# Moving one output-projection tile, the token statistics and the last rope copies to other places in a fused attention and FFN kernel

## What is computed

```python
xn = layernorm(x)
s = attention(xn)        # 16 heads of 32, rope on q and k, causal softmax, output projection Wo
g = silu(ffn(xn))        # bitlinear(w_fc) -> gelu -> bitlinear(w_proj), ternary weights
out = x + s * g
```

## Time and profile before

| what | value |
|---|---|
| median of 3 executions | 1184.5 us (1182.86 to 1184.88) |
| the profiled execution, its own time | 1183.88 us |
| its span, first to last instruction | 1182.2 us |
| PE busy | 1140.4 us, 96% |
| DVE busy | 846.1 us, 72% |
| ACT busy | 792.0 us, 67% |
| POOL busy | 520.4 us, 44% |
| mean granted TensorE clock | 0.999 of full speed |

### The profile page before, as it was taken

How to read it: one execution, slowest core, us unless ns; L and a number is a source line. 1 busy time by engine, 2 the same in 40 slices (tenths; PEclk the granted TensorE clock), 3 DMA queues, 4 the chain that set the end, 5 groups by cost and what they waited for, 6 DMA issues and landing times.

```text
span 1182.2 us, 20037 instructions
## 1 busy us (share of the span) xinstructions
PE 1140.4 (96%) x7580; PEld 559.3 (47%) x7580; DVE 846.1 (72%) x1442; ACT 792.0 (67%) x1492; POOL 520.4 (44%) x894
## 2 busy tenths in 40 slices
PE   4989999999999999999999999999999999999997
PEld 3555545446444454445544454444544445444553
DVE  6988848797558875588547984479745887558854
ACT  4787974578826868269663797447873587826964
POOL 2135442572526625275243744257252562526434
PEclk9999999999999999999999999999999999999999
DMA  8490001910128000450007401092001900045011
GB/s 302 152 125 21 2 29 38 141 55 1 30 30 149 19 3 28 56 123 19 30 1 85 94 19 30 1 122 75 2 30 24 155 19 4 27 53 91 19 39 37
DMA packets 52587, 67.31 MB, mean 57 GB/s; under 512 B 9353, under 2 KB 34313, under 8 KB 51977
## 3 DMA queue, kind: packets, MB, share of 16 engines
q1 hardware_dynamic: 52488, 66.02, 28.3%
HBM read 31.98 MB, written 8.40 MB: 34 GB/s over the span
## 4 chain that ended last, share of the span: by engine, by line
PE 71%; DVE 15%; ACT 6%; POOL 3%; issue 2%; DMA 1%; SPq 1%; POOLq 0%; DVEq 0%; ACTq 0%
PE banks L404 22%; PE banks L561 17%; PE banks L530 12%; PE banks L648 5%; PE banks L617 5%; ACT arena L847 4%; PE banks L509 4%; DVE arena L1104 3%; DVE mix L1080 3%; DVE arena L1102 3%; PE banks L516 2%; DVE mix L983 1%; PE banks L434 1%; ACT banks L825 1%; POOL mix L1290 1%
## 5 line engine op out<-in xcount | busy, mean ns | idle before, releaser
L561 PE MATMUL banks<-projT,arena 128*128 128x512 f16 x1024 | 285.3, 377 | 0.0
L825 ACT ACTIVATE banks<-banks,mix,scl 128x512 f32<-128x512 f32 (+2 forms) x384 | 249.4, 668 | 15.5 <-POOL mix L1290 14.1
L1080 DVE TENSOR_REDUCE mix<-banks 128x1 f32<-128x384 f32 (+3 forms) x352 | 218.9, 637 | 35.9 <-PE banks L516 20.0
L530 PE MATMUL banks<-xT,fcT 128*128 128x512 f16 x1024 | 228.4, 379 | 0.9
L847 ACT ACTIVATE arena<-banks,scl 128x1280 f32<-128x1280 f32 x128 | 164.7, 1328 | 68.9 <-PE banks L617 65.5
L1273 POOL TENSOR_TENSOR split_buf<-xr_buf,split_buf 128x512 f16<-128x512 f32 x64 | 74.0, 1177 | 247.2 <-ACT split_buf L771 247.2
L1282 POOL TENSOR_TENSOR xh_buf<-xh_buf 128x512 f32<-128x512 f32 x120 | 152.3, 1269 | 65.6 <-ACT xh_buf L794 61.9
L404 PE MATMUL banks<-xT,qkT 128*128 128x512 f16 x768 | 168.7, 379 | 0.0
L530 PEld LDWEIGHTS banks<-xT,fcT 128*128 128x128 f16 x1024 | 97.7, 98 | 121.9 <-ACT xh_buf L794 9.8
L1290 POOL TENSOR_SCALAR mix<-mix,scl 128x1 f32<-128x1 f32 (+1 forms) x288 | 76.2, 265 | 153.9 <-DVE mix L1080 144.4
L1053 DVE TENSOR_TENSOR arena<-banks,mix 128x512 f32<-128x512 f32 x128 | 79.4, 682 | 85.1 <-PE banks L404 85.1
(11 more groups left out here) (152 smaller groups left out, 1570.4 us busy)
## 6 DMA issues: line engine op xcount, KB each, us to landing
stacks<-split_buf SPq DMA_DIRECT2D x192, 128.0 KB, 5.1
out_dram<-arena SPq DMA_DIRECT2D x32, 256.0 KB, 3.0
xr_buf<-in_L_attn_x_dram SPq DMA_DIRECT2D x7, 1024.0 KB, 7.2
resid<-in_L_attn_x_dram SPq DMA_DIRECT2D x28, 256.0 KB, 5.0
stacks<-in_L_ffn_w_fc_dram SPq DMA_DIRECT2D x1, 4096.0 KB, 25.2
arena<-in_L_ffn_w_proj_dram SPq DMA_DIRECT2D x1, 4096.0 KB, 14.5
mix<-norm_row SPq DMA_DIRECT2D x8, 256.0 KB, 3.9
xr_buf<-in_L_attn_x_dram SPq DMA_DIRECT2D x4, 256.0 KB, 4.1
```

The costliest lines, as they stand in the source:

```text
L530: mm = pe.matmul(banks[:, UP_BANKS[f % NUB], :], fcT[:, c, f * P:(f + 1) * P], xT[:, part, c, :], start=(c == 0 and part == 0), stop=(c == ...
L561: mm = pe.matmul(banks[:, 6 + t % 2, :], lhs, projT[:, f, :], **ends)
L825: mm = nc.scalar.activation(block, block, ACT.Exp, scale=col(EXP_SCALE), bias=exp_bias[:, i, h0 + k:h0 + k + 1], accum_out=row_sum[:, i, h ...
L1080: nc.vector.tensor_reduce(row_max[:, i, h0:h0 + n], scores_of(r), AX_X, ALU.max).then_inc(max_ready, 1)
```

## The change

It alters when things are issued. No matmul is added or left out. One output tile more (tile 1) goes from `out_projection` to `late_out_projection`, so the queue beside the rounds holds 36 output matmuls in place of 24, and `GIVEN` is worked out anew with a lead of 17 and 20 behind rounds 3 and 4 (batch 0 keeps the old lead). Tiles 1, 2, 3 are scaled behind rounds 4, 7 and 12. POOL adds x to each in two halves, behind rounds 6 and 7, 9 and 10, 14 and 15. The statistics of the next batch stand behind the maxima of rounds 5, 7, 9 and 11, and are joined behind round 12, in batch 0 too. POOL's ten steps start at round 16. In all batches but the first, the last rope pair's copies stand behind GELU 2.

```diff
-OUT_EARLY = 2
+OUT_EARLY = 1
 OUT_BESIDE_SCORES = (NT - OUT_EARLY) * OUT_MATMULS
-STATS_AFTER = (8, 9, 10, 11)
-FIRST_STATS_AFTER = (9, 10, 11, 12)
+LATE_STATS_AFTER = {5: 0, 7: 1, 9: 2, 11: 3}
-NORM_FROM = 8
+NORM_FROM = 16
...
-DOWN_LEAD = (0, 0, 11, 13, 16)
+FIRST_LEAD = (0, 0, 11, 13, 16)
+LEAD = (0, 0, 11, 17, 20)
...
-RESIDUAL_AFTER = {r + 2: t for r, t in SCALED_AFTER.items()}
+RESIDUAL_AFTER = {r + 2 + half: (t, half) for r, t in SCALED_AFTER.items() for half in range(2)}
...
-                    pe.wait_ge(scaled_ready, b * NT + t - 1)
+                    if t >= 2:
+                        pe.wait_ge(scaled_ready, b * NT + t - 1)
...
-                    if f == 0:
+                    if f == (0 if first else 2):
                         split_rotated(3)
...
-                    stats_after = FIRST_STATS_AFTER if first else STATS_AFTER
-                    if f in stats_after and not last:
-                        token_statistics(b + 1, stats_after.index(f))
-                    if f == FC - EARLY - 1 and not last:
-                        join_statistics(b + 1)
...
                 for r in range(EARLY, NR):
                     maxima(r)
+                    if r in LATE_STATS_AFTER and not last:
+                        token_statistics(b + 1, LATE_STATS_AFTER[r])
+                    if r == NORM_FROM - 4 and not last:
+                        join_statistics(b + 1)
...
+            def add_half_of_x(b, t, half):
+
+                cols = slice(half * D // 2, (half + 1) * D // 2)
+                pool.wait_ge(resid_dma[t % 2], b * 32 + 16 * (t // 2) + 16)
+                pool.wait_ge(scaled_ready, b * NT + t + 1)
+                added = nc.gpsimd.tensor_tensor(result[:, t, cols], result[:, t, cols], resid[:, t % 2, cols], ALU.add)
+                if half:
+                    added.then_inc(result_ready, 1)
...
-                    for t in range(2):
+                    for t in range(OUT_EARLY):
                         add_x(b - 1, t)
...
-                        add_x(b - 1, RESIDUAL_AFTER[r])
+                        add_half_of_x(b - 1, *RESIDUAL_AFTER[r])
```

More of the change, by code:

```diff
@@ L64, with given_after_rounds @@
 EXP_COLS = [sum(n * ((i + 1) * P + 412) if i else 940 for i, _, n in ROUNDS[:r + 1]) for r in range(NR)]
-DOWN_LEAD = (0, 0, 11, 13, 16)
-def given_after_rounds(total):
-    return [DOWN_LEAD[r] if r < NSB else DOWN_LEAD[-1] + (total - DOWN_LEAD[-1]) * EXP_COLS[r - NSB] // EXP_COLS[-1] for r in range(NR)]
+FIRST_LEAD = (0, 0, 11, 13, 16)
+LEAD = (0, 0, 11, 17, 20)
+def given_after_rounds(lead, total):
+    return [lead[r] if r < NSB else lead[-1] + (total - lead[-1]) * EXP_COLS[r - NSB] // EXP_COLS[-1] for r in range(NR)]
 def round_behind(given, matmuls):
     return 1 + min(r for r in range(NR) if given[r] >= matmuls)
-FIRST_GIVEN = given_after_rounds(DOWN_BESIDE_SCORES)
-GIVEN = given_after_rounds(OUT_BESIDE_SCORES + DOWN_BESIDE_SCORES)
+FIRST_GIVEN = given_after_rounds(FIRST_LEAD, DOWN_BESIDE_SCORES)
+GIVEN = given_after_rounds(LEAD, OUT_BESIDE_SCORES + DOWN_BESIDE_SCORES)
 FIRST_KEEP_DOWN = tuple(round_behind(FIRST_GIVEN, (t + 1) * DOWN_MATMULS) for t in range(2))
```

## The result

The changed kernel takes 1188.54 us (median of 7, 1187.27 to 1189.17) against 1183.78 us of the kernel before, run beside it. The ratio is 1.0037, with a 95% interval of 1.0025 to 1.0049: slower. The prediction said 1189.3 us against 1184.5, a ratio of 1.0041.

What follows compares the result with a forecast made beforehand. PE, busy 1140.4 of 1182.2 us, was taken as the bound, so only its stalls count. Batches 1 to 6 +3.2, batch 7 +0.7, batch 0 +0.9: +4.8 us, 1189.3 against 1184.5; range 1182.5 to 1193.5, the forecast's own 1186.5 to 1192.

Steps and rivals of the forecast that it cites:

- The forecast case: Whole kernel: 1189.3 us against 1184.5, 0.4% slower, by the sum of PE's stalls; chance 0.60.
- (a): Up projection to round 0, before the change: PE loses 0.38 us per batch, put down to statistics on DVE.
- (b): Round 4, before the change: 0.82 us late per batch, released by a square, put down to statistics on DVE.
- The moved tile at zero: Batches 1 to 7: 12 matmuls (2.59 us) move from ahead of the up projection to beside the rounds; zero by itself.
- Copies behind GELU 2: Up tile 4, batches 1 to 7: the copies make tile 1's square late on ACT, +0.83 us each.
- Stalls (a) and (b) gone: Batches 1 to 6: with the statistics out of the up projection both stalls vanish, together -1.20 us per batch.
- DVE in the pass: Score pass, rounds 4 to 13: 10.2 us of DVE work makes round 18 late, 0.9 us lost per full batch.
- POOL: Score pass: half additions, steps and powers delay biases; 0.9 us lost at round 22, 0.2 from the power at round 21.
- rival 1: Score pass: DVE's backlog is absorbed and the pass's old 1.11 us stall falls to zero; 1176 us, chance 0.10.
- Batch 0: First batch: +0.9 us at round 18, +0.2 by later powers, -0.2 in the up projection; +0.9 in all.
- The transfer of x's tile 3: Load issued about 539.2, landing 4.1 us later, before POOL wants it at 545.1; covered by 1 to 2 us.
- The port rule: Statistics beside POOL's halves might block on a shared port; charged nothing. With a late transfer as rival: +4, 1193, chance 0.13.

Runs made afterwards that it cites:

- run 7: The change with rope copies apart behind two squares, statistics behind rounds 17 to 23, POOL's steps from 28, but output tile 1 and lead put back: 1176.0 us.
- run 8: The kernel before with only the last rope pair's copies moved behind GELU 2: 1200.0 us, ratio 1.0136.
- run 1: The change with the last rope pair's two copies apart, behind the squares of tiles 0 and 1, in all batches but the first: 1183.14 us.
- run 2: The change with only POOL's ten layer-norm steps moved, from round 16 to round 28: 1181.46 us, ratio 0.9977.
- run 3: The change with only the statistics and their join put back in the up projection, behind tiles 8 to 12 (batch 0: 9 to 12): 1186.24 us.
- run 9: The change with both rope copies behind GELU 0 again in every batch: 1189.04 us, ratio 1.0041.

## Why the prediction was right

The forecast case came true, with its mechanism. The range, 1182.5 to 1193.5, held the time, and so did the forecast's own, 1186.5 to 1192. The medians differ by 4.8 us, as forecast. That this agrees to a tenth is partly luck, since single terms are off by about 0.1 us per batch in both directions. Taken from the two traces, the six full batches lose 3.4 us (forecast 3.2), batch 0 1.05 (0.9) and batch 7 0.65 (0.7), 5.1 us of span.

- *Bound.* PE has the same matmuls, so the time moved by PE's stalls. The period came to 141.30 us where 141.2 was said. A full batch is longer by 0.57 us on average, and the stalls of PE down to 0.04 us account for 0.54 of it: +0.83 at tile 4, -1.20 for (a) and (b), and +0.91 in the pass (2.03 for 1.12).
- *The moved tile at zero.* Nearly right for its matmuls (0.16 us in run 7). What I had not priced is that POOL's addition of x moves with it. The kernel before has no stall at tile 7, so there was nothing to win against it. But with the copies behind GELU 2 the moved addition is what keeps tile 7 on time: without it 0.50 us more would be lost in each of seven batches (run 8). The sum had no such term, and that this was right is luck, since the prediction never worked out tile 7.
- *Copies behind GELU 2,* +0.83 us. Measured 0.83 in six of the seven batches (0.28 and 0.55 at tiles 3 and 4 in batch 3, where a rope transfer was late), and by taking it away, 5.4 of 5.8 us (run 1, where 0.26 us at tile 3 of batch 3 remain).
- *Stalls (a) and (b) gone,* -1.20 us. Both are gone. The earlier trace rows shows rounds 3 and 4 of batch 7, and not 4 and 5 as its title and the prediction say: two output matmuls stand between them, and three behind round 4. So the 0.16 us of batch 7 are round 4's own stall without statistics, and of (b)'s 0.82 only 0.66 belong to the statistics; run 7, with the old lead and no statistics there, loses the same 0.16. The sum doesn't change.
- *DVE in the pass,* +0.9. Measured 0.19 + 0.07 + 0.56 = 0.82 (rounds 13, 17 and 18). Its work from round 4 to 13 was 10.12 us for 10.2.
- *POOL,* 0.9 + 0.2. Measured 0.31 + 0.65 + 0.16 = 1.12, and 1.20 with 0.04 at each of rounds 19 and 20. A half cost 0.72 us and not 0.63, the power 1.04 as assumed. The last is at round 32; that it belongs to the power at round 21 is argued, and run 2 shows only that it is the steps'. Run 2 separates the two terms, and run 3 shows that POOL's exists only behind DVE's, as rival 1 had assumed.
- *Batch 0.* It loses 0.12, 0.26, 0.31 and 0.38 us at rounds 14, 15, 17 and 18, where it lost 0.23 at round 18 before, and 0.27 more at round 26: +1.11, for +1.1 forecast in the pass.
- *The transfer of x's tile 3.* It was issued at 682.50 in batch 4 and landed 2.8 us later, not 4.1; POOL wanted it at 688.56.
- *The port rule.* The 32 statistics take 679 to 695 ns, and the one at 680.62 lies beside a half of POOL (680.42 to 681.13) at 0.68 us. So charging nothing for it was right. The Trainium skill, "Advanced Engine Details and Errata", section "VectorE Performance Modes", has GpSimd block VectorE instructions that run in a two-port mode; the traces show no such block for this operation, and not in which mode it runs.

Where the reasoning was thin: x's transfer was dismissed as needed only by round 5. That is true for the change, where x lands 15 us before it is needed, but I did not keep it as a limit for other versions, and runs 3 and 8 ran into it.

## What to carry to other kernels

On an engine with slack but little of it per step, what counts is what stands directly behind an inserted instruction. Behind the result that others wait for, one at a time, the two copies were all but free; in front of it, both together, they cost PE 0.83 us per batch. No run tells the place from the splitting. A move is priced over every queue that it passes: here the copies' place decided when POOL's sums began and when the next x could be loaded, and a stall that is removed can uncover a transfer that had just fitted. Spare time of an engine has to be looked for round by round: DVE had none in the 512-column rounds 4 to 12 once the three scalings stood there (7.5 us of work against PE's 7.4), and 0.2 us in each of the 384-column ones.

## What the runs showed that was not expected

- A transfer of 1 MB issued behind rope copies took 7.8 us to land in batch 4 of run 3 and 8.4 in batch 4 of run 8, and was the limit for statistics at up tile 8 in two runs (1.80 and 1.84 us of DVE idle).
- Halving an addition on POOL from 512 to 256 columns saved 0.54 of 1.26 us, not half.
- The same rope transfers are there at different times in the batches of one execution: run 9 lost nothing at up tile 3 in batch 1, 2.1 us in batch 2 and 0.83 in batch 4.
